# Mixture-of-experts kernel: the first expert's weight applied where the result joins x, late weights loaded earlier, and four smaller edits

## The reference

```python
# first layer's FFN: every token's two best of 8 experts; experts are low-rank additions to shared w1, w3, w2
probs = softmax(t @ gate_w.T);  topw, topi = top_k(probs, 2);  topw = topw / sum(topw)
h1 = t @ w1.T + 2.0 * (t @ a1[e].T) @ b1[e].T          # h3 alike, with w3, a3, b3
act = silu(h1) * h3
out_e = act @ w2.T + 2.0 * (act @ a2[e].T) @ b2[e].T
out = sum(weights[e] * out_e)                           # two experts per token
# first layer's attention: gated linear attention, numerator and denominator by cumulative sums
# second layer's FFN: one expert per token by its best centroid: alpha * (relu(xln @ w1[e] + b1[e]) @ w2[e] + b2[e])
# second layer's attention: softmax
x = x + 0.5 * ffn0(norm(x)); x = x + attn0(norm(x)); x = x + 0.5 * ffn0(norm(x))
x = x + 0.5 * ffn1(norm(x)); x = x + attn1(norm(x)); x = x + 0.5 * ffn1(norm(x))
```

## Time and profile before

| | us |
|---|---|
| median of 3 runs | 1007.69 (1007.35 to 1010.24) |
| profiled execution | 1008.46 |
| its span in the trace | 1006.7 |
| PE busy | 926.1 (92%) |
| DVE busy | 735.5 (73%) |
| POOL busy | 606.1 (60%) |
| ACT busy | 567.9 (56%) |

### The profile page before, as it was taken

The page is one execution under the profiler, slowest core; times in us unless marked ns, Lnnn a source line. Parts: engine busy times, 40 slices in busy tenths (PEclk is TensorE's granted clock), DMA queues, the critical chain, the costliest instruction groups (busy, mean ns, idle before and its releaser), DMA issues. The chain is left out here.

```text
span 1006.7 us, 17622 instructions
## 1 busy us (share of the span) xinstructions
PE 926.1 (92%) x5072; PEld 702.7 (70%) x5072; DVE 735.5 (73%) x2093; ACT 567.9 (56%) x1270; POOL 606.1 (60%) x566
## 2 busy tenths in 40 slices
PE   3899999999999999999999998759999899989996
PEld 2677777776777667776767676429995666757996
DVE  5778788899889798998999888544442567665443
ACT  4544655766857667674565443106663767634664
POOL 4777678868577586775867876614443135453443
PEclk9999999999999999999999999969999999999999
DMA  6890000000000000000000000136564000004552
GB/s 175 342 391 1 1 1 0 1 1 1 1 1 1 1 1 1 2 0 1 11 1 11 12 1 12 45 140 183 173 182 136 1 13 22 20 28 136 176 176 91
DMA packets 39775, 62.74 MB, mean 62 GB/s; under 512 B 7074, under 2 KB 23266, under 8 KB 37505
## 3 DMA queue, kind: packets, MB, share of 16 engines
q1 hardware_dynamic: 35136, 53.08, 16.1%
q0 software_dynamic: 4544, 8.54, 2.5%
HBM read 34.68 MB, written 27.82 MB: 62 GB/s over the span
## 5 line engine op out<-in xcount | busy, mean ns | idle before, releaser
L382 PE MATMUL bank<-split 128*128 128x512 f32 x544 | 244.4, 449 | 9.4 <-DVE ud L1340 3.6
L384 PE MATMUL bank<-split 128*128 128x512 f32 x544 | 215.2, 396 | 0.0
L383 PE MATMUL bank<-split 128*128 128x512 f32 x544 | 213.8, 393 | 0.0
L895 ACT ACTIVATE sil<-bank 128x512 f32<-128x512 f32 x128 | 76.0, 595 | 146.6 <-PE bank L384 145.8
L382 PEld LDWEIGHTS bank<-split 128*128 128x128 f32 x544 | 103.2, 190 | 41.0 <-issue 10.0
L1286 DVE TENSOR_TENSOR act<-act,wT 128x512 f32<-128x512 f32 x128 | 123.7, 966 | 4.4
L383 PEld LDWEIGHTS bank<-split 128*128 128x128 f32 x544 | 103.6, 190 | 26.3 <-issue 10.5
L1282 DVE TENSOR_TENSOR act<-bank,sil 128x512 f32<-128x512 f32 x128 | 87.9, 686 | 44.2 <-issue 20.8
L384 PEld LDWEIGHTS bank<-split 128*128 128x128 f32 x544 | 102.9, 189 | 23.8
L1742 POOL TENSOR_TENSOR act<-act 128x512 f32<-128x512 f32 x64 | 86.7, 1354 | 30.5 <-DVE act L1286 30.4
L1748 POOL TENSOR_TENSOR split<-act,split 128x512 fp32r<-128x512 f32 x64 | 92.8, 1451 | 18.1 <-ACT split L964 17.9
(11 more groups left out here) (308 smaller groups left out, 2039.8 us busy)
## 6 DMA issues: line engine op xcount, KB each, us to landing
...
rows_in<-yw,slot_i POOLq DMA_INDIRECT x64, 2.3
rows_out<-ob,ids POOLq DMA_INDIRECT x39
out<-ob,ids POOLq DMA_INDIRECT x39
```

The costliest lines, as they stand in the source:

```text
L382: mm(dst, w[0], m[0], start=start, stop=False, **more)
L383: mm(dst, w[0], m[1], start=False, stop=False, **more)
L384: return mm(dst, w[1], m[0], start=False, stop=stop, **more)
L895: af(sil[(k - 1) % 2][:, :], bank[BH1[STEPS[k - 1][0] % 2]][:, :], ACT.Silu).then_inc(silu_done.sem, 1)
```

## The change

1. **Weights.** With w0 and w1 the weights of a token's two experts, the main part now computes act0 + act1 x (w1/w0), and f_add multiplies the result by w0/2. ACT saves `half_w` = w0/2 per token (three buffers; it waits for the f_add of the item three before). DVE takes its reciprocal (`slot_ratio`, between `act(3)` and `act(4)`), PE transposes it as before, and ACT's `mask(2)` saves it as 0.5 times itself less 1, which is w1/w0. `mask(3)` is gone. `act(k)` multiplies by the weight for e = 1 only. `f_add` is four instructions with a scalar per partition.
2. **Late weights.** SP's wait for POOL's memset is gone, and with it the memset; the biases eb2r are now split in pieces of 8 rows on DVE (`bias_parts`). The four loads of e2 stand behind the first three e1 loads and have a semaphore of their own, for which PE waits before the tiles.
3. **Denominators** by transposes.
4. **Table loads.** ACT executes Silu on one column right behind the constants, and Exp on one column behind `tiles(0)`.
5. **Fills.** 20 behind the constants, 3 and 4 in the slot of the first item's `q`.
6. **Registers.** PE's `experts(...)` stands at the start of `expert`, no longer ahead of the bias matmul.

```diff
@@ -106 +106 @@
         tT = sb("tT", [P, S])
-        mx = sb("mx", [P, 4, T]); dlt = sb("dlt", [P, T]); th = sb("th", [P, T]); wts = sb("wts", [P, T])
+        mx = sb("mx", [P, 4, T]); dlt = sb("dlt", [P, T]); th = sb("th", [P, T]); wts = sb("wts", [P, T]); half_w = [sb(f"half_w{i}", [P, T]) for i in range(3)]
         oh = [sb(f"oh{i}", [P, T, E, R], BF16) for i in range(2)]
         mT0 = sb("mT0", [P, S]); mT1 = [sb(f"mT1{i}", [P, S]) for i in range(2)]; mdT = [sb(f"mdT{i}", [P, S]) for i in range(2)]
-        wT = [[sb(f"wT{i}{k}", [P, S]) for k in range(2)] for i in range(2)]
+        wT = [sb(f"wT{i}", [P, S]) for i in range(2)]
         ua, ud = [sb(f"ua{k}", [P, S]) for k in range(2)], [sb(f"ud{k}", [P, S]) for k in range(2)]
@@ -214 +214 @@
         late_loads += [(eb2r[k:k + E, :], d["eb2"].rearrange("o (n p) -> (o n) p", p=P)) for k in (0, 64, 96)]
-        late_loads += [(e2[:, n:n + 2, :, :], d["e2"][:, n:n + 2, :, :]) for n in range(0, E, 2)]
+        e2_loads = [(e2[:, n:n + 2, :, :], d["e2"][:, n:n + 2, :, :]) for n in range(0, E, 2)]
@@ -333 +333 @@
                     sp.wait_ge(*h3_ready(MAINS - 1))
-                    sp.wait_ge(zeroed.sem, 8)
                     for dst, src in late_loads:
@@ -348 +347 @@
                     matrix(first + t, slice(t, t + 1))
+                if call == 0:
+                    for dst, src in e2_loads:
+                        sp.dma_start(dst, src).then_inc(e2_loaded.sem, 16)
                 for i in range(4):
@@ -386 +388 @@
                     mm(bank[0][:, :], ident_bf[:, :], oh[0][:, :, :, :].rearrange("p t e r -> p (t e r)"), start=True, stop=True)
+
+            def warm_up(count):
+                for _ in range(count):
+                    mm(bank[0][:, :].rearrange("p (t d) -> p t d", t=T), ident_bf[:, :], ident_bf[:, :].unsqueeze(1).to_broadcast([P, T, P]),
+                       start=True, stop=True)
@@ -433 +440 @@
                     for j in js:
-                        pe.wait_ge(*weighted(g, STEP[j, 0]))
+                        pe.wait_ge(*act_done(g, STEP[j, 0]))
                         last = mm(bank[BV][:, :], a2[:, j, :], act0[j][:, :], start=j == 0, stop=j == J - 1)
@@ -528 +535 @@
                     for t in range(T):
-                        last = mm(bank[BSIDE][:, t:t + 1], den[0:1, rows(t)], ones[0:1, 0:1], start=True, stop=True)
+                        last = tr(bank[BSIDE][:, t:t + 1], den[0:1, rows(t)], ident[0:1, 0:1])
                     last.then_inc(den_ready.sem, 1)
@@ -654 +661 @@
                 h(1, 2)
+                if q == 0:
+                    warm_up(3)
                 logits()
...
                     up(0); up(1)
+                    warm_up(4)
                 down(l, 2)
@@ -711 +721 @@
             def expert(n0, n1, n2):
+                if n2 is not None:
+                    e = experts(pe, kept, n2)
                 if n1 is not None:
@@ -729 +741 @@
                 if n2 is not None:
-                    p, e = n2 % 2, experts(pe, kept, n2)
+                    p = n2 % 2
                     out_rows = bank[4 + p][:, 0:P]
@@ -843 +855 @@
             pe.wait_ge(*constants(0))
+            warm_up(20)
             for s in SLOTS:
@@ -851 +864 @@
             pe.wait_ge(*eb2_steps(0))
+            pe.wait_ge(e2_loaded.sem, 16 * len(e2_loads))
             pe.wait_ge(*tabs_ready(0))
@@ -927 +941 @@
                     act.wait_ge(*tanh_done(q))
-                    af(wts[:, :], th[:, :], ACT.Copy, scale=-0.5, bias=0.5).then_inc(slot_w.sem, 1)
+                    act.wait_ge(*xf_done(q - 3))
+                    af(half_w[q % 3][:, :], th[:, :], ACT.Copy, scale=-0.25, bias=0.25).then_inc(slot_w.sem, 1)
...
                         return
-                    if n < 3:
-                        act.wait_ge(*maskT_ready(q, n + 1))
-                    else:
-                        act.wait_ge(*maskT_saved(q, 3))
+                    act.wait_ge(*maskT_ready(q, n + 1))
                     if n == 0:
...
                         act.wait_ge(*weighted(q - 2))
-                    dst = (mT0, mT1[q % 2], *wT[q % 2])[n]
-                    if n < 3:
+                    dst = (mT0, mT1[q % 2], wT[q % 2])[n]
+                    if n < 2:
                         ins = af(dst[:, :], bank[BPRE][:, :], ACT.Copy)
                     else:
-                        ins = af(dst[:, :], wT[q % 2][0][:, :], ACT.Copy, scale=-1.0, bias=1.0)
+                        ins = af(dst[:, :], bank[BPRE][:, :], ACT.Copy, scale=0.5, bias=-1.0)
                     ins.then_inc(maskT_saved.sem, 1)
@@ -1101 +1113 @@
                 mask(2)
-                mask(3)
                 a_gate(0)
@@ -1228 +1239 @@
             act.wait_ge(*constants(0))
+            af(nmx[:, 0:1], ones[:, :], ACT.Silu)
             for s in SLOTS:
...
             tiles(0, 2, expert)
+            af(nmx[:, 1:2], ones[:, :], ACT.Exp)
             act.wait_ge(*ob_ready(NT - 1))
@@ -1280 +1293 @@
                     v.tensor_tensor(a[:, :], bank[BH3[j % 2]][:, :], sil[(k - 1) % 2][:, :], ALU.mult).then_inc(act_done.sem, 1)
+                    if e == 0:
+                        return
                     dve.wait_ge(*act_done(g, k))
-                    if k == 1:
+                    if j == 0:
                         dve.wait_ge(*maskT_saved(g))
-                    v.tensor_tensor(a[:, :], a[:, :], wT[g % 2][e][:, :], ALU.mult).then_inc(weighted.sem, 1)
+                    v.tensor_tensor(a[:, :], a[:, :], wT[g % 2][:, :], ALU.mult).then_inc(weighted.sem, 1)
+
+                def slot_ratio():
+                    if q is None:
+                        return
+                    dve.wait_ge(*slot_w(q, 1))
+                    v.reciprocal(wts[:, :], half_w[q % 3][:, :]).then_inc(slot_w.sem, 1)
@@ -1365 +1386 @@
                     dve.wait_ge(*back_ready(l))
-                    v.scalar_tensor_tensor(xc(l), tok(bank[BOUT][:, :]), 0.5, xc(l), ALU.mult, ALU.add).then_inc(xf_done.sem, 1)
+                    for t in range(T):
+                        last = v.scalar_tensor_tensor(xc(l)[:, t, :], bank[BOUT][:, rows(t)], half_w[l % 3][:, t:t + 1], xc(l)[:, t, :],
+                                                      ALU.mult, ALU.add)
+                    last.then_inc(xf_done.sem, 1)
@@ -1449 +1473 @@
                 r_top1(s.r_sort)
+                slot_ratio()
                 act(4)
@@ -1611 +1636 @@
                     v.tensor_copy(pick_bf[k:k + 32, :], ident[k:k + 32, k:k + E])
-                chain(v.tensor_copy(eb2p[:, :], eb2r[:, :]), 1)
-                chain(v.tensor_tensor(eb2r[:, :], eb2r[:, :], eb2p[:, :], ALU.subtract), 2)
-                chain(v.tensor_copy(eb2p[64:P, :], eb2r[64:P, :]), 3)
-                chain(v.tensor_tensor(eb2r[64:P, :], eb2r[64:P, :], eb2p[64:P, :], ALU.subtract), 4)
-                v.tensor_copy(eb2p[96:P, :], eb2r[96:P, :]).then_inc(eb2_steps.sem, 1)
+                chain(v.memset(eb2p[:, :], 0.0), 1)
+                for k in (0, 64):
+                    v.tensor_copy(eb2p[k:k + E, :], eb2r[k:k + E, :])
+                chain(v.tensor_copy(eb2p[96:96 + E, :], eb2r[96:96 + E, :]), 2)
+                v.tensor_tensor(eb2r[64:64 + E, :], eb2r[64:64 + E, :], eb2p[64:64 + E, :], ALU.subtract)
+                chain(v.tensor_tensor(eb2r[96:96 + E, :], eb2r[96:96 + E, :], eb2p[96:96 + E, :], ALU.subtract), 3)
+                v.tensor_copy(eb2p[64:64 + E, :], eb2r[64:64 + E, :])
+                chain(v.tensor_copy(eb2p[96:96 + E, :], eb2r[96:96 + E, :]), 4)
+                chain(v.tensor_tensor(eb2r[96:96 + E, :], eb2r[96:96 + E, :], eb2p[96:96 + E, :], ALU.subtract), 5)
+                v.tensor_copy(eb2p[96:96 + E, :], eb2r[96:96 + E, :]).then_inc(eb2_steps.sem, 1)
@@ -1738 +1768 @@
                         return
-                    pool.wait_ge(*weighted(g, STEP[j, 1]))
+                    pool.wait_ge(*weighted(g, j + 1))
                     pool.tensor_tensor(out=act1[j][:, :], in0=act0[j][:, :], in1=act1[j][:, :], op=ALU.add).then_inc(summed.sem, 1)
@@ -1934 +1964 @@
                     pool.memset(zrow, 0.0).then_inc(zeroed.sem, 1)
-                if s.m == MAINS:
-                    pool.wait_ge(*h3_ready(MAINS - 1))
-                    pool.memset(eb2r[:, :], 0.0).then_inc(zeroed.sem, 1)
             tiles(0, 3, expert)
```

28 lines of the change are left out of this document (14 added, 14 removed).

## The result

The changed kernel takes 969.33 us (median of 4 runs, 967.97 to 970.89), the kernel before, in 4 runs beside it, 1008.68. The ratio is 0.9612 (95% interval 0.9596 to 0.9628): 39 us or 3.9% faster. The forecast was 967.4. The profiled execution has a span of 969.1 us, 37.6 less than before.

The account below looks back on a forecast made before the run. The prediction took PE to bound the loop, its removable time being PE's own waiting and work. Its terms summed to -40.25 us: 1008.46 less 40.25 is 968.2, less 0.77 gives 967.4 us; range 955 to 984.

Parts of the forecast that it names:

- B: First layer's token loop: DVE's relief removes most PE waits that DVE ended, and a half-clock dip; -13.8 us.
- A: Start: two table loads leave ACT's path and fills bring PE to full speed sooner; -3.7 us.
- E: Handover to the second layer's experts: no DMA wait, first tile 4.33 us behind the last scatter; -13.1 us.
- F: First softmax: Exp's table load moves behind the tiles, so PE's 0.57 us wait goes; -0.6 us.
- G: Expert tiles: PE's register loads at the step's start leave 0.3 us idle each instead of 0.62; -4.5 us.
- C: Denominators, eight chunks: transposes instead of fp32 matmuls save PE 0.62 us each; -5.0 us.
- D: Last chunk's f_add, before statistics and attention: four instructions' extra 0.67 us shows with some cover; +0.45 us.
- relief passed on: Rival in the loop: DVE's relief passes to other waits, on POOL or ACT; 978 us, chance 0.15.
- The handover's clock: Rival at the handover: half the gain, tokens or tables late or PE's clock still falling; 974.5 us, chance 0.09.
- The register window: Rival at the expert tiles: register loads exposed, sequencer held 1.5 us before the next four matmuls; 986 us, chance 0.06.
- The drain behind a table load: Rival on ACT: each removed load brings its first steps 1.4 us earlier still; 963.3 us, chance 0.03.
- slower case: Rival in the loop: DVE's reciprocal waits for ACT's half weights, stalling 16 slots; 1015 us at 3 us each, chance 0.02.

Follow-up runs that it names:

- only_weights: The kernel before with the change of the weights alone; late weights, denominators, table loads, fills and registers as before: 992.58 us, ratio 0.9836.
- denominators_matmul: The changed kernel with the denominators turned by four fp32 matmuls again: 976.72 us, ratio 0.9661.
- one_add: The changed kernel with f_add as one 128x512 instruction with constant 0.5, leaving out the tokens' weights there (another result): 969.26 us, ratio 0.9598.
- late_both_back: The changed kernel with the late weights again waiting for POOL's memset and the second-layer matrices' loads back in their batch: 984.54 us, ratio 0.9743.
- no_early_tables: The changed kernel without the early one-column Silu and the early one-column Exp: 972.69 us, ratio 0.9626.
- registers_old_place: The changed kernel with PE's register load back between the transpose and the bias matmul: 974.97 us, ratio 0.9654.
- dummy_multiply: The changed kernel with DVE multiplying each of the first expert's activations by itself into an unread spare tile, 64 times: 994.13 us, ratio 0.9859.
- no_start_fills: The changed kernel without the 27 fills at the start: 971.69 us, ratio 0.9630.
- late_wait_back: The changed kernel with POOL's memset and SP's wait for it put back, the second-layer matrices' loads staying behind: 975.11 us, ratio 0.9663.

## Why the prediction was right, point by point

The forecast of 967.4 us and the range held, since the two large terms had the right mechanism. The sum was -40.25 us, the profiled spans differ by 37.6. Part of the closeness is luck: B gave 2.6 us more than its term, and A, E, F and G together some 5 less, so their errors cancel in part. The terms:

| term | predicted | measured | from |
|---|---|---|---|
| A, start | -3.7 | -2.6 | before and changed; 48.1 to 49.9 in the variants |
| B, weights in the loop | -13.8 | -16.4 | only_weights: loop -15.7, its end -0.7 |
| C, denominators | -5.0 | -4.7 | denominators_matmul |
| D, last addition | +0.45 | +0.44 | PE's wait behind it: 0.89 before, 1.33 changed, 0.90 one_add |
| E, handover | -13.1 | -12.3 | before and changed, -11.8 with D in it; late_both_back 11.6 |
| F, Exp's table | -0.6 | -0.1 to -0.2 | no_early_tables |
| G, registers | -4.5 | -2 to -4 | before and changed -1.9; registers_old_place 4; between the means of the kernels with either place, from the first tile on, -3.0 with F |

**A** had nearly the right size by the wrong causes. It gave 1.35 us to the first table load, 1.3 to the second and 1 to the clock. The experiments show nothing for the fills, and for both tables 0.4 us against the changed kernel (49.40 and 49.01), where kernels that are alike differ by 1.8. only_weights, which has none of these, begins its loop 1.7 us earlier than the kernel before. There ACT has one mask less and DVE fewer multiplies while the pipeline fills. PE's wait for the mask, 1.58 us in the earlier trace rows, is 0.73, and of its waits between 30 us and the loop, 2.3 in all, 0.7 are left. Which of the two, mask or multiplies, does it was not run. The step that failed is "the first load was wholly on the path": it was on the path to the first transposes, which do come 1.6 us earlier, and as far as the second chunk's, 1.4 us earlier in the changed kernel than in no_early_tables. From there to the second chunk's gate matmuls 1.0 of it was lost, where PE's granted clock came back 0.8 us later. The wait for POOL that grew from 1.94 to 3.02 us took back what the fills had gained and nothing of this: without fills it is 1.88.

**B** had the mechanism: dummy_multiply shows that the loop's time follows DVE's, and the waits for z and ud were the ones that went. The size was low by 2.6 us. I counted the waits as listed, and PE's idle time did fall by 11.3 us in only_weights (15.6 to 4.3), near the 12.1 taken. But PE's busy time fell by 4.4 too, and I had only 1.7 of it, the dip of the clock, which is gone as forecast. Of the other 2.7 a part is the longer first matmul behind a wait (0.50 us, where one behind another of its kind takes 0.39), which goes with the wait; I haven't accounted for all of it.

**D** held, and in its place. It meant the last chunk's addition, behind the loop, on which PE waits by way of `nxt`. The kernel before, the changed kernel and one_add have there:

```profile
642.62 1.03 PE L551 MATMUL bank<-cen,xnT 128*128 128x8 f32 x8 [0.89 <-DVE nxt L1533]
```

```profile
619.35 1.03 PE L558 MATMUL bank<-cen,xnT 128*128 128x8 f32 x8 [1.33 <-DVE nxt L1558]
```

```profile
617.83 1.03 PE L558 MATMUL bank<-cen,xnT 128*128 128x8 f32 x8 [0.90 <-DVE nxt L1555]
```

What the term left out is the loop, where one_add prices the four parts at another 0.8; with DVE still what PE waits for, the expectation of one_add had it at 3.7.

**C** held to 0.3 us.

**E** held in its parts: no DMA wait, the last scatter as the next late event, and 4.49 us from there to the first tile where 4.33 were taken from call 1. The term took the last scatter at its old place. It stands 26.6 us behind the loop's last f32r matmul in the changed kernel and 25.4 in the kernel before, 1.1 us more. Some 0.4 of it is D. In this stretch PE's granted clock is at half from 620.6 to 624.0. In dummy_multiply, no_start_fills and no_early_tables it isn't, the scatter stands at 25.7 to 25.8 and the handover is 0.6 to 0.8 us shorter. (In one_add, without the dip and without D, it is 25.3, as before.) The wait of 1.33 us before the dip stands in the kernels without it too; why the clock falls in some and not in others stays open. No rival asked which of the two edits does it. They cover for each other: either alone leaves 5 us or nothing of the 11.6.

**F** failed at "no PE wait at the first Exp": the 0.57 us for the first softmax piece did go, but PE now stands 0.30 us for the second one, for which ACT itself waits for DVE.

**G** is the term with the wrong reading. 9.9 us of idle time at the weight load isn't PE's idle time: the waits of PE itself before the bias matmul, in the view of PE's waits after the first tile, are 5.6 us in 15. Of the new place the prediction said 0.3 us of idle each, and 4.5 us in 14 stand there. In the changed kernel's waits after the first tile:

```profile
PE bank L735 <- ACT hT_e L1172: 4.5, 14, 0.5
PE bank L735 <- ACT xlT L1165: 2.2, 4, 0.6
```

The sign that the prediction named for G, the waits at the two matmuls together below 6 us, failed: they are 7.6, all at the first matmul, and were 8.7 before. So the move shortened the stop only a little. The price of the load was off too: in the trace of the kernel before its eight further instructions are some four of 146 ns and four of 18, 0.66 us in all and not 1.2. The rest of what it gives is partly a change of segment: the last load of a call now stands before the last transpose and not behind it, which moves 0.8 and 0.9 us from the segments "end" and "second layer" into those of the tiles, and the tiles did not get longer by it.

The rivals: relief passed on did not happen (PE's idle time in the loop is 4.7 us under any name). The handover's clock did not fall in the changed kernel at the fills (full from 624.0 on), though PE stands 1.05 us there for the tokens. It does fall in late_wait_back, but behind the 3.35 us for the late weights and not at the last scatter, which that rival had named. The register window was not exposed at 1.5 us. The drain behind a table load that the Trainium skill gives ("ScalarE: Activation LUTs", What ACT_TABLE_LOAD costs) has no trace here: in no_early_tables, too, the ACTIVATE starts 1.29 us behind the load, and taking the load away gave less than the load's own 1.28. The reciprocal that was to be the slower case waited 0.3 us for ACT once in the whole execution.
